# A cross-attention and mixture-of-experts layer: where the rows of the second last batch are scattered, and what moves with them

## The reference

```
x = x + attention(layernorm(x), ctx)     # 16 heads of 16, q from x, k and v from ctx, softmax, projection wo, biases
x = x + ffn(layernorm(x))
ffn:  probs = softmax((x @ Wg + bg) / 5)          # 8 experts
      vals, idx = top_k(probs, 2);  gates = vals / (sum(vals) + 1e-9)
      y = sum over the 2 chosen experts of  gate * (gelu(x @ W1[e] + b1[e]) @ W2[e] + b2[e])   # 256 -> 512 -> 256
```

## Time and profile before

| what | us |
|---|---|
| median of 3 runs | 809.06 (807.59 to 813.81) |
| the profiled execution | 810.81 |
| its span, first to last instruction | 808.9 |
| PE busy in the span | 757.3 (94%) |
| DVE busy | 610.6 (75%) |
| ACT busy | 455.7 (56%) |
| POOL busy | 394.6 (49%) |

### The profile page before, as it was taken

One profiled execution on the slowest core, in us unless ns is written; L12 is line 12 of the kernel. 1 busy time (PEld: TensorE's weight loads), 2 busy tenths in 40 slices (PEclk: granted clock), 3 DMA queues, 4 the chain that ended last, 5 costly groups with the idle time before them and its releaser, 6 DMA issues.

```text
span 808.9 us, 16337 instructions
## 1 busy us (share of the span) xinstructions
PE 757.3 (94%) x4672; PEld 452.5 (56%) x4672; DVE 610.6 (75%) x1126; ACT 455.7 (56%) x663; POOL 394.6 (49%) x357
## 2 busy tenths in 40 slices
PE   9999999999999999999999888769999989999994
PEld 4443344444444444444444333348999879989994
DVE  6787778798798797788787787646777877766773
ACT  2066676775776776766766655843345434444441
POOL 6506143547647637728725603343453555344443
PEclk9999999999999999999999999999999999999998
DMA  6765857757757657757767556876454455454441
GB/s 220 208 180 175 224 169 219 226 170 257 209 177 251 208 191 241 202 178 229 209 176 244 163 160 239 287 266 118 77 94 78 84 129 104 71 78 74 72 70 12
DMA packets 90660, 136.24 MB, mean 168 GB/s; under 512 B 15456, under 2 KB 49216, under 8 KB 90192
## 3 DMA queue, kind: packets, MB, share of 16 engines
q1 hardware_dynamic: 76592, 117.33, 48.1%
q0 software_dynamic: 13296, 17.09, 12.0%
q10 hardware_dynamic: 688, 0.79, 0.3%
HBM read 71.25 MB, written 64.04 MB: 167 GB/s over the span
## 4 chain that ended last, share of the span: by engine, by line
PE 75%; issue 6%; ACT 6%; DVE 5%; DMA 4%; POOL 2%; another core or an unknown queue 0%; SPq 0%; DVEq 0%; POOLq 0%
PE ps_pv L1544 13%; PE ring L1710 10%; PE ring L1692 10%; PE ring L1531 10%; PE ring L1518 7%; PE ps_x L1575 7%; ACT probs L1022 4%; DMA out<-y_sb,xs 4%; PE ps_x L1595 4%; PE ring L1701 3%; PE ps_x L1585 3%; PE ps_x L1605 2%; DVE negm L1094 2%; PE ps_pv L1683 1%; PE ps_x L1562 1%
## 5 line engine op out<-in xcount | busy, mean ns | idle before, releaser
L1094 DVE TENSOR_REDUCE negm<-ring 128x2 f32<-128x1024 f32 x256 | 310.3, 1222 | 75.4 <-PE ring L1518 66.0
L1022 ACT ACTIVATE probs<-ring 128x1024 f32<-128x1024 f32 x256 | 260.2, 1024 | 94.1 <-PE ring L1531 73.0
L910 POOL DMA_INDIRECT out<-y_sb,xs x71 | 110.2, 1553 | 142.8 <-DMA out<-y_sb,xs 87.8
L1544 PE MATMUL ps_pv<-probs,v_aug 128*32 128x512 f32 x1024 | 137.2, 608 | 5.7 <-ACT probs L1022 5.7
L1531 PE MATMUL ring<-kq 64*128 64x512 f32 x512 | 126.2, 492 | 7.3 <-DVE negm L1094 6.1
L1518 PE MATMUL ring<-kq 64*128 64x512 f32 x512 | 106.1, 413 | 10.8 <-ACT probs L1022 6.2
L1531 PEld LDWEIGHTS ring<-kq 64*128 64x128 f32 x512 | 47.5, 183 | 110.5 <-issue 76.2
L1055 ACT CAST xsT_hi<-ps_pv 128x256 fp32r<-128x256 f32 x70 | 26.1, 373 | 132.8 <-PE ps_pv L1683 125.2
L801 POOL DMA_INDIRECT xs_dram<-xg,rows x64 | 63.5, 993 | 55.5 <-DVEq L1262 30.8
L1710 PE MATMUL ring<-w_hi,hT_hi 128*128 x284 | 85.3, 300 | 0.1
L1710 PE MATMUL ring<-w_lo,hT_hi 128*128 x284 | 80.1, 282 | 0.0
(11 more groups left out here) (197 smaller groups left out, 1222.4 us busy)
## 6 DMA issues: line engine op xcount, KB each, us to landing
kq<-k_dram SPq DMA_DIRECT2D x64, 192.0 KB
kq<-q_dram SPq DMA_DIRECT2D x64, 192.0 KB
xs<-xs_dram SPq DMA_DIRECT2D x71, 132.5 KB
k_dram<-qk_hi SPq DMA_DIRECT2D x32, 256.0 KB
q_dram<-qk_hi SPq DMA_DIRECT2D x32, 256.0 KB, 2.7
o_dram<-oT SPq DMA_DIRECT2D x32, 256.0 KB
w_dram<-w_sb SPq DMA_DIRECT2D x12, 512.0 KB
w_hi<-w_dram SPq DMA_DIRECT2D x12, 512.0 KB
```

What stands on the lines that cost most here:

```text
L910: pool.indirect_dma_start(out=out, out_offset=bass.IndirectOffsetOnAxis(ap=xs[j % AHEAD][:, TOKEN:TOKEN + 1].bitcast(I32), axis=0), in_=y_ ...
L1022: nc.scalar.activation(probs[kt][:, 2 * jp:2 * jp + 2, :], ring[PLACE["ST", u, p] % RINGS][:], ACT.Exp).then_inc(exp_done, 1)
L1094: nc.vector.tensor_reduce(negm[:, v % 2, :, jp, kt], ring[PLACE["MX", v, p] % RINGS][:], AX.X, ALU.max, negate=True).then_inc(max_free, 1)
L1544: mm = nc.tensor.matmul(ps_pv[2 * DH * j:2 * DH * (j + 1), :], v_aug[:, kt, HPG * g + j, :], probs[kt][:, j, :], start=(kt == 0), stop=(kt ...
```

## The change

1. In bodies' last two groups (u = 30, 31: `late`) `pv` stands behind the scores of p = 3, 5, 7 instead of 2, 4, 6, and the last quarter of group 30 at p = 1 of group 31; `take_o(30)` moves along.
2. In body 7, for batch 6: XG0 from (2,5) to (2,7), XG1 from (2,6) to (3,0), LG from (2,7) to (3,1), the router's exponential from (3,0) to (3,3), its four steps from (3,1)..(3,4) to (3,4)..(3,7). PX and `route_rows` go from (3,5) behind the body to tile 0. For batch 5, "second" goes from (0,3) to (0,4) and "gates" from (0,4) to (0,6).
3. The scatter of batch 6 goes from the end of the body to tiles 1 to 8, one indirect DMA ahead of each `add_out`.
4. `normalise(7, 0)` goes from (3,6) to tile 2.
5. x of batch 7 is fetched into `xgT` instead of `xg`. `bring_x` waits for LG of batch 6 instead of its scatter, and stands ahead of `put_recip(7, 1)` and `fetch_o(7, 1)` on SP. The XG copies of batch 7 now wait for the store of that x; `apply_last` waits for the scatter instead.
6. `last_tables` is cut into eight parts at tiles 27 to 34; its instructions are the same.

```diff
 LAST_POST = {(1, 3): "OP0", (1, 4): "OP1", (1, 5): "OP2", (1, 6): "OP3",
-             (2, 5): "XG0", (2, 6): "XG1", (2, 7): "LG", (3, 5): "PX"}
+             (2, 7): "XG0", (3, 0): "XG1", (3, 1): "LG"}
...
-LAST_ROUTE = {(0, 1): "softmax", (0, 2): "first", (0, 3): "second", (0, 4): "gates"}
-LAST_ROUTE_POST = {(3, 1): "softmax", (3, 2): "first", (3, 3): "second", (3, 4): "gates"}
+LAST_ROUTE = {(0, 1): "softmax", (0, 2): "first", (0, 4): "second", (0, 6): "gates"}
+LAST_ROUTE_POST = {(3, 4): "softmax", (3, 5): "first", (3, 6): "second", (3, 7): "gates"}
...
-TAIL_PE = {6: "OP0", 7: "OP1", 8: "OP2", 9: "OP3", 17: "XG0", 18: "XG1", 19: "LG", 25: "PX", 26: "CN"}
+TAIL_PE = {0: "PX", 6: "OP0", 7: "OP1", 8: "OP2", 9: "OP3", 17: "XG0", 18: "XG1", 19: "LG", 25: "PX", 26: "CN"}
...
-TAIL_TABLES = {27: "tiles", 28: "past", 29: "rows"}
-TAIL_RECIP, TAIL_NORMALISE, TAIL_APPLY, TAIL_EXP, TAIL_POW, TAIL_SCATTER = 1, 5, (15, 16), 20, 13, 25
+TAIL_TABLES = {27 + n: n for n in range(8)}
+TAIL_NORMALISE = {2: 0, 5: 1}
+TAIL_RECIP, TAIL_APPLY, TAIL_EXP, TAIL_POW, TAIL_SCATTER = 1, (15, 16), 20, 13, 25
+TAIL_SCATTER_BEFORE = 1
...
+def tail_batch(j):
+    return B - 2 if j == 0 else 1 if TAIL_PE[j] == "CN" else B - 1
+def late(u):
+    return u >= G - 2
...
-            return x_of(b) if b < B - 1 else xg[:, :, 0:D]
+            return x_of(b) if b < B - 1 else xgT[:].rearrange("p c s -> p (c s)").rearrange("p (t d) -> p t d", d=D)
...
             def bring_x(b):
                 sp.wait_ge(x_moved, 16)
-                sp.wait_ge(scattered, 16 * TOPK * NT * b)
+                sp.wait_ge(full["LG"], b)
                 settle(sp, passed_sp)
-                sp.dma_start(xg[:, :, 0:D], out_tiles[:, b * NT:(b + 1) * NT, :]).then_inc(x_moved, 16)
+                sp.dma_start(sum_of(b), out_tiles[:, b * NT:(b + 1) * NT, :]).then_inc(x_moved, 16)
...
+            bring_x(B - 1)
             put_recip(B - 1, 1)
             fetch_o(B - 1, 1)
-            bring_x(B - 1)
...
-                if i == B - 1:
-                    scatter(i - 1)
...
             for j in range(TILES):
                 if j == TAIL_POW:
                     ln2(B - 1)
+                if j == TAIL_SCATTER_BEFORE:
+                    rows_ready(B - 2)
+                if TAIL_SCATTER_BEFORE <= j < TAIL_SCATTER_BEFORE + TOPK * NT:
+                    scatter_tile(*divmod(j - TAIL_SCATTER_BEFORE, NT))
...
+                    if b == B - 1:
+                        act.wait_ge(out_done, 16 * B)
                     nc.scalar.copy(xgT[:, int(name[2]), :], ps_x[:]).then_inc(done[name], 1)
...
-                        if p == 0 and u > 0:
+                        if u > 0 and p == (1 if late(u - 1) else 0):
                             take_o(u - 1)
...
             def apply_last(b, half):
                 dve.wait_ge(rstd2_done, b + 1)
-                dve.wait_ge(out_done, 16 * (b + 1))
                 dve.wait_ge(full["XG1"], b)
+                dve.wait_ge(scattered, 16 * TOPK * NT * b)
...
-                        if (g, p) == (3, 6):
+                        if (g, p) == (3, 6) and not last:
                             normalise(i, 0)
...
-                        if p == 0 and u > 0:
+                        if u > 0 and p == (1 if late(u - 1) else 0):
                             pv(u - 1, NT - 1)
-                        if p in (2, 4, 6):
-                            pv(u, p // 2 - 1)
+                        if p in ((3, 5, 7) if late(u) else (2, 4, 6)):
+                            pv(u, (p - 2) // 2)
...
                 if j == 0:
-                    pe.wait_ge(done["PX"], B - 1)
+                    pe.wait_ge(done["LG"], B - 1)
```

More of the change, by code:

```diff
@@ L1030, in body @@
                                 misc(name, b)
-                        if (g, p) == (3, 0) and i == B - 1:
+                        if (g, p) == (3, 3) and i == B - 1:
                             route_exp(i - 1)
@@ L1328, in last_tables @@
                 tiles = tile_no[:, 0:n]
-                if part == "tiles":
+                if part == 0:
                     dve.wait_ge(done["CN"], 2)
@@ L1334, in last_tables @@
                     c2.link(v.tensor_scalar(n_sh[:], n_up[:], P.bit_length() - 1, None, ALU.arith_shift_right))
+                elif part == 1:
                     c2.link(v.tensor_copy(n_tiles[:], n_sh[:]))
@@ L1338, in last_tables @@
                     c2.link(v.tensor_tensor_scan(ends[:], ones_e[:], left_n[:], 0.0, ALU.mult, ALU.add))
+                elif part == 2:
                     c2.link(v.tensor_tensor(start[:], left_n[:], ends[:], ALU.subtract))
@@ L1343, in last_tables @@
                     c2.link(v.tensor_tensor(step[:, 0:E - 1], start[:, 1:E], start[:, 0:E - 1], ALU.subtract))
-                elif part == "past":
+                elif part == 3:
                     c2.link(v.tensor_tensor(past[:, 0:n], tiles.unsqueeze(2).to_broadcast([P, n, E]), spread(ends[:], n), ALU.is_ge))
                     c2.link(v.tensor_tensor(past_n[:, 0:n], past[:, 0:n], spread(left_n[:], n), ALU.mult))
+                elif part == 4:
                     c2.link(v.tensor_reduce(e_of[:, 0:n], past[:, 0:n], AX.X, ALU.add))
                     c2.link(v.tensor_reduce(first_of[:, 0:n], past_n[:, 0:n], AX.X, ALU.add))
+                elif part == 5:
                     c2.link(v.tensor_tensor(past_n[:, 0:n], past[:, 0:n], spread(step[:], n), ALU.mult))
                     c2.link(v.tensor_reduce(start_of[:], past_n[:, 0:n], AX.X, ALU.add))
-                else:
+                elif part == 6:
                     c2.link(v.tensor_scalar(e_tab[:, TILES1:], e_of[:, 0:n], float(E - 1), None, ALU.min))
                     added_before(TILES1, n)
+                else:
                     c2.link(v.tensor_scalar(live[:], e_of[:, 0:n], float(E), None, ALU.is_lt))
@@ L1450, in tail @@
                     reciprocals(b, 1)
-                if j == TAIL_NORMALISE:
-                    normalise(b, 1)
+                if j in TAIL_NORMALISE:
+                    normalise(b, TAIL_NORMALISE[j])
                 if j in TAIL_PE and TAIL_PE[j][:2] != "XG":
-                    misc(TAIL_PE[j], 1 if TAIL_PE[j] == "CN" else b)
+                    misc(TAIL_PE[j], tail_batch(j))
                 if j in TAIL_LN2:
@@ L1737, in _ @@
                 if j in TAIL_PE:
-                    misc(TAIL_PE[j], 1 if TAIL_PE[j] == "CN" else B - 1)
+                    misc(TAIL_PE[j], tail_batch(j))
             output(TILES - 1, e[TILES - 1])
```

## The result

The changed kernel takes 807.02 us in the median (803.85 to 815.1, 20 runs) where the kernel before takes 810.76 us beside it: a ratio of 0.9954, 95% interval 0.9934 to 0.9973. Run again in two later comparisons it gave 0.9921 (0.9887 to 0.9954) and 0.9949 (0.9927 to 0.9970). The three have a mean of 0.9941, so the change brings some 4.8 us of 810, and the forecast was 8.2. The direction was right. The size was not, and 807.0 lies above the range's 805.5.

A forecast was written before the change was run, and what follows sets the result against it. PE was taken as the bound, busy 757.3 of 808.9 us. Start 4.1, scatter -0.1, tables 4.0 and route steps 0.2 sum to 8.2 us, so 809.06 becomes 800.9, range 796.5 to 805.5.

The forecast's parts named there:

- The start: Last groups to first tiles: tile 4's turn_x 4.1 us earlier, though PE could start hidden(0) 6.5 us earlier.
- Rival C: At the start no transfer holds: PE 6.5 us earlier, clock kept (+1), tables 4.35; 11.9 us in all, 797.2; chance 0.18.
- A: At the start transfers hold almost everything: w2_hi loads or oT's stores end only 1 us earlier; 803.9 us; chance 0.18.
- The queue's part: Row loads of tile 4 issued 3.7 us earlier: 2.7 from the scatter's bytes leaving, 1.0 from SP's waits.
- the 1 us of slack: Tile 4's turn_x stood 3.0 us behind its row load's issue, up to 1 us of it slack; 0.4 taken.
- The scatter beside the tiles: Tiles 1 to 8: scatters run while POOL would idle, their transfers delay the first serial adds; cost 0.1 us.
- rival B: Tiles 1 to 8: the scatter throttles the adds, 6.2 us per add, 18.4 us lost; 819.3 us, slower; chance 0.08.
- The tables: Tiles 27 to 34: eight steps fit DVE's free 0.9 us a tile, removing most of a 4.35 us stall; gain 4.0.
- Rival D: Tiles 28 to 35: the tables' stall is only spread out, giving back 4; gain 4.2 us, 804.9; chance 0.10.
- The route steps: Batch 5's second and gates later, where PE waited 1.62 us for a maximum: gain 0.2 us, bounds -0.5 and 1.

The follow-up runs named there:

- before_route: The kernel before with only batch 5's router steps moved (second to (0,4), gates to (0,6)); ratio 1.0012 (0.9991 to 1.0033).
- scatter2_late: The changed kernel with batch 7's scatters two to a tile before adds 32 to 35; one execution, 796.89 us.
- after_third: The changed kernel as it is, run again in a later comparison; 796.53 us, ratio 0.9949 (0.9927 to 0.9970) to the kernel before.
- paced_pads: The changed kernel with batch 7's scatters at tiles 25, 26, 28, 29, 31, 32, 34, 35 and pads at row loads 39 to 41; 792.46 us, ratio 0.9902.
- after_3tables: The changed kernel with the tables in three steps as before; 805.38 us, ratio 0.9936 (0.9908 to 0.9963) to the kernel before.
- after_again: The changed kernel as it is, profiled and timed once more; 803.07 us, ratio 0.9921 (0.9887 to 0.9954) to the kernel before.
- before_late_norm: The kernel before with only late values in groups 30 and 31 and normalise(7, 0) at tile 2; ratio 0.9994 (0.9973 to 1.0014).

## Why the prediction was right or wrong

**The start, 4.1 us: right.** Over ten profiles with the change's start, MT of group 30 to turn_h(2) takes 37.6 us in the mean (36.4 to 38.9); in the three of the kernel before's start 41.5: 3.9 us. Hidden(0) came 6 to 7 us earlier, 22.0 in the mean instead of 28.1 to 29.8, and 3.9 of it came through; that is the forecast's "not 6.5 us come through". Rival C (no transfer holds, 6.5) falls by that, and A (1 us) too. The queue's part, 3.7 us at the row loads, is less sure: they stand at 37.5 to 38.3 us in three of the four profiles with the scatter in that stretch, but at 35.7 in before_route, and at 34.0 to 36.3 in the ten without. The means differ by 2.3 us. The Trainium skill (DMA: Bandwidth & Descriptors, Issuing engines are not separate DMA queues) has transfers of all engines share the DMA engines; the direction agrees, the size is below the 2.7 us of bytes alone plus 1.0. That the row loads of this profile came at 539.30 against 539.5 was in part luck: two shares that were each off by over 1 us the opposite way made up the sum, 2.3 and 1.5 where 1.0 and 2.7 stood. The forecast left out the wait for tile 0's gelu (1.9 us) and the half clock behind it; that the 1 us of slack took them is argued, not tried.

**The scatter beside the tiles, 0.1 us: right in kind, and rival B is dead.** It costs nothing: tiles 2 to 13 take 41.57 us in most profiles, PE all busy. Three of the ten profiles with the change's start take more, 41.99, 42.39 and 42.92. In the kernel after they were even 1.1 us shorter than before, which I had not foreseen. Y_sb's longest wait, 2.34 us, became 1.2 in the kernel after; that this is the reason was not tried by itself. The forecast charged 0.9 us of transfer to each scatter between waiting adds, from the 4.95 us of the last two adds of the earlier trace rows (by count they are adds 24 and 25, not 25 and 26). That reading was wrong: in scatter2_late the same two adds are 5.03 us apart with no scatter between them. The scatter instruction took 0.98 to 1.00 us beside the adds in seven of eight cases and 1.23 in one; the stall of a VectorE operation of some 0.7 us each that the Trainium skill (SBUF — State Buffer, Who interferes with whom) would allow isn't there.

**The tables, 4.0 us: the step that failed.** The prediction put it: "in eight tiles that is 0.9 each, just the free time", with bounds 3 and 4.35. Of DVE's work this was right: tiles 29 to 31 lost their stall. But the sum asked only whether DVE had the time, and not what is late next. Those tiles hold the scatter of batch 7 and the pads beside adds that wait for each other, and y_sb(31) waits for the landing of add 29: 1.35 us in the kernel after, in a step of 6.10 us instead of 3.46. By ratios the edit brings 0 us on the kernel before and 1.2 on the changed one; by tiles 28 to 36 it brings 0.9 on the kernel before (32.06 to 31.12) and 0.9 on the changed one (32.69 to the mean of the three, 31.82; after_third's 32.63 holds a stretch of 3.4 us at half clock). That is the 3 to 4 us that are missing from 8.2. With the traffic moved (paced_pads) the same eight tiles take 28.98, 3.7 less than after_3tables. So something near the term's size could be had, but not by the tables' edit alone; how much of the 3.7 the moved traffic would bring with the tables in three steps was not tried. Rival D (804.9, a ratio of 0.9949) named the size, but for another reason: DVE's steps spread over the tiles would make them all 3.9 us. Three steps of 3.9 us are there and hold 1.3 us of what the eight tiles lose, but the one of 6.1, behind an add, holds the other 2.6; and two of the three were gone in paced_pads (3.48 and 3.52) with the tables' steps as they were.

**The route steps, 0.2 us:** nothing, inside the bounds.

**Sum:** 3.9 for the start, 1.1 at tiles 2 to 13, 0.9 for the tables, 0 for the route make 5.9; measured, by the ratios, are 3.7, 6.4 and 4.1 us in three comparisons, 4.8 in the mean. The sum by the profiles lies above it, and I have no account for the difference.

## What to carry to other kernels

Before a stall is taken out, list what else goes on during it. Transfers and a chain of dependent DMAs that got through in its cover are late next, and a sum over the stalled engine's free time does not see them. Here they had to be moved as well: neither the first spread of the pads nor the paced scatters alone brought a gain that could be measured; both moved together made the gain 8.1 us where the changed kernel had 4.1 beside it. And a transfer's own place in the list counts twice: the pads stood beside the adds and ahead of a row load.

## What the runs showed of the hardware that was not expected

An indirect add of 128 rows into DRAM holds its buffer for 4 to 6 us: y_sb(31) started 4.10 us behind add 29 in paced_pads, with no pad write in flight beside it, and 4.07 to 6.22 us behind it in the nine with pads in flight there (the eight table steps in all ten). An add that has to wait for the landing of the one before started 5.03 us behind it in scatter2_late with neither a scatter nor a pad beside it (624.94 to 629.97). At a ring of two buffers 1.3 us more (5.39 against 4.10) was enough to hold three engines. The granted clock fell to 1.2 GHz for stretches of 3.4 us or more behind waits of PE, in other places from profile to profile: at 533.9 in after, behind a wait of 1.88 us; nowhere but at the end in after_again; for 10.2 us from 505.3 on in before_late_norm, behind one of 2.47 us. By the matmuls' 0.43 us instead of 0.23 such a stretch of 3.4 us costs about half its length where PE is busy, some 1.6 us (an estimate). So one stretch more or less can hide or feign a gain of that size in a single profile; the stages had to be read over many.
